# Causal attention with each mask product cut to its own 64 output rows, so that the four products of a pair of heads use the four quarters of the array

## The reference

```python
# first layer
scores = jnp.einsum('bqhd,bkhd->bhqk', q, k) / jnp.sqrt(jnp.float32(D))
causal = jnp.tril(jnp.ones((T, T), dtype=bool))
scores = jnp.where(causal, scores, jnp.float32(-1e+30))
p = jax.nn.softmax(scores, axis=-1)
y = jnp.einsum('bhqk,bkhd->bqhd', p, v).reshape(B, T, C)
# second layer: the same form, masked by -inf
att = jax.nn.softmax(scores, axis=-1)
out = jnp.einsum('bhlm,bmhd->blhd', att, v)
```

```python
q = l2norm(q) * qs
q = q * cos * scale + rotate_half(q) * sin * scale
```

## Time and profile before

| | |
|---|---|
| time, median of 3 runs | 5112.9 us (5112.71 to 5128.32) |
| the profiled execution | time 5118.15 us, span 5116.4 us |
| TensorE | busy 4646.9 us (91% of the span), granted clock 0.965 on average |
| VectorE, ScalarE, GpSimd busy | 3793.6, 2777.4, 2074.1 us |
| the four mask products of a call (L841) | 4096 products in all, in the two causal attentions |

### The profile page before, as it was taken

The page is one execution under the profiler, slowest core; times in us unless marked ns, Lnnn a source line. Parts: engine busy times, 40 slices in busy tenths (PEclk is TensorE's granted clock), DMA queues, the critical chain, the costliest instruction groups (busy, mean ns, idle before and its releaser), DMA issues. The chain is left out here.

```text
span 5116.4 us, 170069 instructions
## 1 busy us (share of the span) xinstructions
PE 4646.9 (91%) x75792; PEld 2835.7 (55%) x75792; DVE 3793.6 (74%) x4462; ACT 2777.4 (54%) x3791; POOL 2074.1 (41%) x1499
## 2 busy tenths in 40 slices
PE   7858997998789869999999999999999999999998
PEld 5623334444333346674766566655676567746664
DVE  5667883333778568886988589868997689869895
ACT  4527774223477745555555455555555556545554
POOL 4330000001000046654666366635664466536661
PEclk9979997999799989999999999999999999999999
DMA  0021111000111121111111111111111111111110
GB/s 23 12 69 32 44 43 34 1 0 27 58 40 41 29 63 40 40 36 47 40 39 39 42 41 41 37 44 39 40 40 52 26 40 40 40 43 40 40 40 26
DMA packets 95786, 192.97 MB, mean 38 GB/s; under 512 B 27088, under 2 KB 45520, under 8 KB 93264
## 3 DMA queue, kind: packets, MB, share of 16 engines
q1 hardware_dynamic: 95056, 182.09, 13.9%
HBM read 60.36 MB, written 15.73 MB: 15 GB/s over the span
## 5 line engine op out<-in xcount | busy, mean ns | idle before, releaser
L1848 POOL TENSOR_TENSOR part_of_layer<-part_of_layer,sine_of_layer 128x512 f32<-128x512 f32 x768 | 963.4, 1276 | 629.6 <-DVE sine_of_layer L1720 629.6
L1855 POOL TENSOR_TENSOR part_of_layer<-part_of_layer,inverse_of_layer 128x1024 f32<-128x1024 f32 x384 | 730.7, 1903 | 324.9 <-ACT inverse_of_layer L1603 309.9
L967 ACT ACTIVATE prob_of_ca<-ps 128x1024 f32<-128x1024 f32 (+3 forms) x768 | 594.2, 814 | 262.0 <-PE ps L841 196.4
L1717 DVE TENSOR_TENSOR part_of_layer<-ps,rope 128x1024 f32<-128x1024 f32 x384 | 466.0, 1214 | 35.3 <-ACT square_of_layer L1591 32.7
L1720 DVE TENSOR_TENSOR sine_of_layer<-ps,rope 128x1024 f32<-128x1024 f32 x384 | 464.1, 1209 | 0.0
L1634 ACT ACTIVATE values_of_layer<-ps 128x1024 f32<-128x1024 f32 x192 | 196.6, 1024 | 492.4 <-PE ps L1490 492.4
L859 PE MATMUL ps<-keys_of_ca,queries_of_ca 64*128 64x512 bf16 (+3 forms) x1536 | 331.1, 342 | 132.8 <-DVE top_of_ca L999 60.8
L1509 PEld LDWEIGHTS ps<-prob_t_of_layer,mixed_of_layer 64*64 64x64 f32 x12288 | 339.3, 135 | 162.9 <-issue 153.3
L1416 PE MATMUL ps<-qkv,shifted 128*128 128x512 f32 x768 | 384.4, 623 | 27.8 <-POOL values_of_layer L1858 20.2
L1760 DVE TENSOR_REDUCE total_of_layer<-prob_of_layer 128x16 f32<-128x1024 f32 x192 | 234.2, 1220 | 234.3 <-ACT prob_of_layer L1627 234.3
L1520 PE MATMUL ps<-heads_out_of_layer,wo 128*128 128x128 f32 x3072 | 385.6, 280 | 13.7 <-ACT heads_out_of_layer L1623 13.0
(11 more groups left out here) (206 smaller groups left out, 9217.4 us busy)
## 6 DMA issues: line engine op xcount, KB each, us to landing
mixed_of_layer<-values_of_layer SPq DMA_DIRECT2D x636, 128.0 KB
mixed_of_layer<-values_of_layer SPq DMA_DIRECT2D x264, 64.0 KB
queries_of_ca<-q_parts SPq DMA_DIRECT2D x384, 32.0 KB
keys_of_ca<-k_parts SPq DMA_DIRECT2D x384, 32.0 KB
qkv<-in_qkv SPq DMA_DIRECT2D x6, 1536.0 KB, 6.6
q_parts<-parts_of_ci SPq DMA_DIRECT2D x16, 384.0 KB, 2.6
k_parts<-parts_of_ci SPq DMA_DIRECT2D x16, 384.0 KB, 2.6
rope<-in_rope SPq DMA_DIRECT2D x6, 1024.0 KB, 9.1
```

What stands on the lines that cost most here:

```text
L967: nc.scalar.activation(prob[:, i % 2, 2 * two:2 * two + 2, j:], ps[:, 2 * two:2 * two + 2, j:], ACT.Exp, scale=scale).then_inc(raised, 1)
L1717: nc.vector.tensor_tensor(part[:, t % 2, side], by_head(slot), table(2 * side, t), ALU.mult).then_inc(parts, 1)
L1848: nc.gpsimd.tensor_tensor(out, out, sine[:, side, :, (1 - to) * half:(2 - to) * half], ALU.add).then_inc(rotated, 1)
L1855: nc.gpsimd.tensor_tensor(part[:, t % 2, side], part[:, t % 2, side], by, ALU.mult).then_inc(scaled, 1)
```

## The change

Each of the four products of a `masks` call takes only the 64 columns of the identity that belong to its own half of the mask, and writes only the 64 output partitions of that half. The zeros are no longer added. Head and half now pick one of the four quarters of the array (row half by head, column half by part). The number of products, their order, the 128 columns that stream through each, and every wait stay as they are; so do the instructions of the other engines.

The other edit scales the tables `rope` by 1024 and gives the logarithm of the squared lengths a factor of 1024 squared inside the activation instruction that is already there, which takes the factor out again. No instruction is added or widened by it.

```diff
                 def masks(first, second, after):
 
                     for part in range(2):
+                        at = slice(part * ROW_HALF, (part + 1) * ROW_HALF)
                         for h, to in enumerate((first, second)):
-                            last = nc.tensor.matmul(to, k["ident_2"][half_of(h), part, :], k[after][half_of(h), part, :],
-                                                    start=False, stop=part == 1)
+                            last = nc.tensor.matmul(to[at, :], k["ident_2"][half_of(h), part, at], k[after][half_of(h), part, :],
+                                                    start=False, stop=True)
                     return last
...
-                    nc.scalar.activation(root[:, t % 2], length[:, t % 2], ACT.Ln).then_inc(logged, 1)
+                    nc.scalar.activation(root[:, t % 2], length[:, t % 2], ACT.Ln, scale=LENGTH_SCALE ** 2).then_inc(logged, 1)
...
-    c["rope"] = np.ascontiguousarray(np.stack([m.astype(f).reshape(TILES, P, DH).transpose(1, 0, 2) for m in tables], 1))
+    c["rope"] = np.ascontiguousarray(np.stack([(m * f(LENGTH_SCALE)).astype(f).reshape(TILES, P, DH).transpose(1, 0, 2) for m in tables], 1))
```

More of the change, by code:

```diff
@@ L49 @@
 LEAST_SQUARE = 1e-24
+LENGTH_SCALE = 1024.0
 LOG_AND_EXP = "natural_log_exp_and_others"
```

## The result

The changed kernel takes **5283.34 us** (median of 4 runs, 5275.6 to 5323.6) against 5115.12 us for the kernel before: a ratio of **1.034 [1.030, 1.038]**, slower. The forecast was 5213 us, with a range up to 5263: the direction was right, the size too small by some 70 us, and the result lies outside the range. Times and ratios are those of fast runs; of the changed kernel's second set of runs (experiment 8) one, 5357.14 us at a granted clock of 0.940, is slow and is left out. The profiled execution has a span of 5278.4 us, 162.0 more than before.

A forecast was written before the change was run, and what follows sets the result against it. Causal groups were taken as a chain changing hands, TensorE limiting masked units; dearer mask calls add 3.2 us a group (28.55 to 31.8), 50 us a stage, 100 us in both: 5213 us, range 5148 to 5263 us.

The forecast's parts named there:

- What bounds the kernel: Causal attentions: no engine is full; TensorE is the limit in masked units, VectorE's reductions in units 4 to 7.
- the free change: Rival at mask calls: changing form between 64*128 and 64*64 costs nothing; 5076 us, chance 0.06.
- the serial pairs: Rival at mask calls: quarters overlap only by pairs, 0.05 us more a call; 5263 us, chance 0.05.
- the idle time that takes up all: Rival in causal groups: TensorE's 3.2 us idle absorbs all it can, only 1.1 us shows; 5148 us, chance 0.05.
- The term of 0.01 us for issuing two more products: In a mask call on TensorE: added to the 0.055 us stream of four quarters running at once.
- 30 x 0.05 taken as 1.6: Extra us a group if quarters overlap only by pairs, 0.05 us more a call; 25 us a stage.
- Sum of a call on TensorE: 0.14 us more: Mask call where TensorE is the limit: 0.095 + 0.01 + 0.055 + 0.095 = 0.255 us against 0.115.
- the price of a change: Array form changes on TensorE around a mask call: 0.095 us each, two a call.
- 24 x 0.14 ... less 0.35: Per group: 24 calls in TensorE's gapless row cost 3.36 us, less 0.35 hidden at units 1 and 2.
- 6 x 0.04: Per group: six calls where another engine waits for the result but TensorE has time afterwards, 0.04 us more each.
- the clock: Rival in masked units: TensorE's pauses cost the full clock, some 20 us a group double, over 500 us; chance 0.02.

The follow-up runs named there:

- experiment 8: Changed kernel plus filling products behind each turn of the rows: 5276.29 us with 20, 5255.21 us with 12; the changed kernel beside the latter 5287.07 us.
- experiment 1: Kernel before with only the scaled tables and the factor in the logarithm, masks unchanged: 5114.43 us, ratio 0.999.
- experiment 2: Kernel before with its four mask products issued twice in the old 64*128 form: 5208.43 us, ratio 1.017.

## Why the prediction was wrong

*What bounds the kernel:* right. The causal attentions changed, the long stage didn't (experiment 1), and TensorE's time in the masked units carries the loss (experiment 2).

*The change's mechanism:* right. Every entry and exit of 64*64 costs, four quarters do run at once, and the free change, the serial pairs and the idle time that takes up all have fallen as rivals. The term of 0.01 us for issuing two more products had no row behind it in the prediction; the starts after bear it out (four within 0.01 us). Two small roundings in the prediction, 30 x 0.05 taken as 1.6 instead of 1.5 and the ends of its own range, move no bound by more than 5 us.

*The step that failed first*, a size and not the mechanism, is "Sum of a call on TensorE: 0.14 us more". It took the price of a change from the distance to the first product behind it, and took that product's own time from a product in the middle of a run. It measured **0.17 us**: the first products of 64*64 are 0.024 us slower and the first of 64*128 0.01 us. This stood in the earlier trace rows, where the first eight quarter products last 0.32 us and start 0.13 us before the next eight, which last 0.30; the prediction passed over that difference. The sum of the call, with 0.024 and 0.01 added, is 0.095 + 0.01 + 0.055 + 0.024 + 0.095 + 0.01 = 0.289 against 0.115: the measured 0.17.

*The second* is "24 x 0.14 ... less 0.35" and "6 x 0.04" per group. With 0.17, and 0.07 for the six calls whose result is waited for (the slower product lies before it), the same count gives 24 x 0.17 + 6 x 0.07 - 0.35 = 4.15, where the prediction had 3.25 and 4.37 was measured. So the count of calls and places was nearly right, and the one term carried 0.9 of the 1.1 us a group; the other 0.2 us stays open. Over 28 groups the 4.37 instead of 3.2 are 33 us: the forecast's 100 would have been some 130.

*The third* is the clock, to which I gave 0.02 and only in the form of a lasting fall over 500 us. It came as short falls: in the profiled execution nine of them, which cost about 24 us in steady groups (eight by 1.4, one by 12.9), and some 5 us more in the second causal attention, whose first group took 38.55 us in the half clock of the start, where the first one's took 33.18. The evidence that I set against it, the last group of the kernel before, which kept its clock, has no turn of the rows and changes its form only around `weigh`; it was no evidence for the middle of the stage. What the falls cost differs from run to run: in the profiled execution of 5310.9 us (experiment 8) the two stages took 26 us more than in this one, with three falls of 27 to 34 us instead of one.

The sum in the profiled execution: the two stretches from first to last exponential grew by 159 us. Of these 24 are the falls and 5 the start of the second causal attention, which leaves 130 for the rest, 122 of them in 28 steady groups of 4.37; the other 3 of the 162 lie around the stages.

The range, up to 5263 us, had room for either miss alone and not for both. Its upper end was the price of serial quarters, which did not come, so that the mis-sized call (30 us) fell inside it by luck; with no falls the kernel stays inside, as the 5255 us with 12 filling products show. The clock carried the time out, and the sum had put it at nothing.

What stays open: why TensorE's clock falls at that wait only when the stretch around it is full of changes of form, and why a call's first products are slower. The runs show that filling the wait stops the falls and that more products between the changes don't; they don't separate the length of the wait from the pauses ahead of it.

## What to carry to other kernels

Use quarters of the array for a run of products and not for one short call between products of another form: the same four mask instructions cost 0.17 us more a call between 64*128 neighbours and 0.055 us less between 64*64 ones. Price a change of form by the distance across it *and* by the duration of the first product behind it. And before cutting rows that are only zeros, look whether columns can be cut: that changes no form and gave 19 us for one added line.

## What the runs showed of the hardware that was not expected

- The first products after a change of form are slower: 0.024 us in 64*64 (four last 0.25 us between 64*128 neighbours, 0.23 us between their own), about 0.01 us in 64*128 (a pair of 128 columns lasts 0.23 instead of 0.22). The starts say the same: the next four quarters begin 0.08 us behind the first four, and 0.055 us behind when nothing changed.
- Four products on the four quarters start within 0.01 us and take the time of one, also when two of them write one bank: a call between its own neighbours takes 0.055 us, in 64*128 0.11.
- The granted clock fell to half (2.4 to 1.2 GHz) for 3.4 to 34.1 us at a time in the middle of stages whose steady groups show TensorE busy 30.0 of 32.9 us; 12 small products in one wait of each group took the clock from 0.90 and 0.98 to 1.00 over the two stages, and the median from 5287 to 5255 us.
